# A pre-norm attention layer and a feed-forward layer on one core: work around chunk, batch and up-stage borders in another order

## The chip, the cores and the metric

The kernel runs on 1 core of one Trainium2 chip. The metric is the device time of one execution in microseconds (us), as the median of several runs. The engines are named as the profile names them: PE is TensorE (matrix products; PEld is its weight load), DVE is VectorE, ACT is ScalarE, POOL is GpSimd, and SP is SyncE, which here only issues DMAs.

## The reference

Two batches of 2048 rows of width 1024, float32 throughout. First a single-head attention layer of width 256 with a residual, then a feed-forward layer with a residual:

```python
x = x + attn(layernorm(x), Wqkv, bqkv, Wo, bo)      # qkv: 1024 -> 3*256; softmax(q k^T / 16) v; Wo: 256 -> 1024
x = x + ffn(layernorm(x), gate_w, up_w, down_w, fc1_w, fc2_w, expert_w, ln_gamma, ln_beta)
# ffn(h): relu(h @ up_w)**2 @ down_w                                   (1024 -> 2048 -> 1024)
#         + (h @ fc1_w @ expert_w * sum(top_2(h @ gate_w))) @ fc2_w    (1024 -> 512 -> 512 -> 1024)
#         then a layer norm with ln_gamma and ln_beta
```

## The kernel before, in words

Each float32 operand is split into a high half (an fp32r cast, made by ACT) and a low half (source minus high half, made by DVE or POOL, lines 1184 and 1922, called `low` on both), and PE sums three products for each operand pair (`mm3`, lines 2146 to 2148). The text calls the two halves the high half and the low half. No scheduler decides the order: the program of every engine is written out by hand, each engine takes its instructions strictly in that order, and semaphores join them (`w.wait_ge`). Every wait therefore also holds up all that stands behind it on its engine, and the same is true of SP, which issues nearly all DMAs.

**Stage 1, chunks (0 to 345 us).** The 4096 rows are taken in 8 chunks `c` of 512. For a chunk DVE computes the norm's statistics (`stats1`, `aggr1`, `diff1`, `rstd1`, with two small PE products between them, `combine1a` and `combine1b`), scales the 16 row groups (`norm1`) and transposes the chunk in eight slabs `j` (`turn1`). ACT makes the high half of a slab (`slab_hi`), DVE or POOL the low half (`slab_low`; slab 0 on DVE, slab 1 on POOL). PE multiplies the eight slabs into Q and K, then makes V in four steps `t`. Only when step 3 of V has read slab 0 may the next chunk's slab 0 be written. Next to all this run the weight sums (`prep`): 40 pieces of 512 KB are loaded, added and subtracted on DVE and POOL, and stored (`ups`, `downs`), for the fast matrix products of the feed-forward layer, which replace eight block products by seven.

**Stage 2, attention (to some 794 us).** 16 pairs `C` of 128-row tiles, `even = 2C` and `odd = 2C + 1`: scores (`s_unit`), row maxima and exponentials, a transpose on DVE (`turn_p`, `turns`), a shuffle through DMA (`shuffle`), P times V (`pv`), the output product (`wo_half`), `residual` (DVE) into the one pair of buffers `x1t`, which `store1` (SP) writes to DRAM as `x1d` and `norm2` (POOL) normalises into `x2n`, stored by `store2`. `residual` of a pair thus waits for `store1` and `norm2` of the pair before. Pairs 0 to 7 belong to one batch, 8 to 15 to the other; at C = 7 and 8 K and V of the second batch are loaded (`load_k`, `load_v`). PE's `pv(7, 0)` waits for `residual(6, 0)`, since both use PSUM bank 6.

**Stage 3, feed-forward (from 794 us).** 4 blocks `n` of 1024 rows; each has an up stage of 70 slots `s` and a down stage of 70 (60 in the last block). Each slot is twelve PE products of 512 columns, with one weight tile that goes through a ring of three: SP fetches it three slots ahead (`fetch`, into `stf`), ACT casts it, POOL makes its low half (`w_low`). In a down stage ACT and DVE (or POOL) also make the two halves of one hidden tile a slot (`hop_hi`, `hop_low`, tiles `hr`), and POOL adds hidden tiles (`h_add`, line 2006) in slots 3 to 36; in the last block DVE adds them (line 1486). The rows of the next block are loaded in two halves (`load_x2`) and transposed by DVE (`turn2`), the second half in slots 44 to 51 of the down stage. `add_beta` on POOL adds beta to the stored residual rows.

The order inside a DVE wait is what matters at most of the places; for the slab and for the PSUM bank it is:

```python
w.wait_ge(*v_turn[c, j])                 # ACT, slab_hi: the slab is transposed
if c:
    w.wait_ge(*p_v[c - 1, 3, j])         # and V, step 3, has read the slab before
...
w.wait_ge(*d_x1[i][g - 2])               # DVE, residual: the store of the pair before has landed
w.wait_ge(*g_x2[g - 2])                  # and POOL has normalised it
```

## Time and profile before

| | us |
|---|---|
| median of 3 runs (lowest, highest) | 2382.38 (2382.31, 2389.34) |
| the profiled execution's own time | 2392.45 |
| its span, first to last instruction | 2390.6 |
| PE busy, share of the span | 2319.8 (97%) |
| DVE, POOL, ACT busy | 1769.4 (74%), 1564.7 (65%), 902.2 (38%) |
| mean granted PE clock, of full speed | 0.990 |

The profile is one execution. Busy time of an engine is the time in which it has an instruction in work; an idle time in square brackets stands before an instruction and names what ended it. The granted clock of PE is given as a share of full speed: 1.0 is 2.4 GHz and 0.5 is 1.2 GHz, and a value between is a mean over a stretch. The DMA share is the mean busy share of the core's 16 DMA engines.

### The profile page before, as it was taken

Reading aid. Unit: us, or ns where it says so; the run is one execution under the profiler, and the core shown is the slowest. Engines: PE = TensorE matmul, PEld = TensorE weight load, DVE = VectorE, ACT = ScalarE, POOL = GpSimd, SP = SyncE. Lnnn points to the kernel's source line nnn. Section 1 sums busy time; section 2 is a strip of 40 time slices with the busy share of each in tenths; the row PEclk is TensorE's granted clock in tenths of the full one; section 3 lists DMA queues with packets and bytes.
Section 4 is the critical chain, followed back from the end, with each engine's and each line's share of the span. In section 5 each row is a group of like instructions: output and inputs, shape, how many; then the busy total and the mean of one; then the engine's idle time right before and its main releaser. Section 6 shows DMA issues by size and latency. Waiting matters only on the chain.

```text
span 2390.6 us, 31307 instructions
## 1 busy us (share of the span) xinstructions
PE 2319.8 (97%) x11224; PEld 1931.4 (81%) x11224; DVE 1769.4 (74%) x2952; ACT 902.2 (38%) x1698; POOL 1564.7 (65%) x1173
## 2 busy tenths in 40 slices
PE   7999999998999999999999999999999999999998
PEld 6888889987888788877887887887787778877786
DVE  5989957887887653854689875479895457989968
ACT  4222233432433353444432444442254343244352
POOL 4557525664665776598658479846649974866763
PEclk9999999999999999999999999999999999999999
DMA  9899846778767733435335343535534443544342
GB/s 244 281 308 283 255 130 194 216 216 278 220 204 215 225 115 93 124 97 146 101 117 179 106 131 92 149 95 158 149 104 117 125 115 110 181 147 131 88 139 87
DMA packets 215802, 386.48 MB, mean 162 GB/s; under 512 B 19552, under 2 KB 95456, under 8 KB 215008
## 3 DMA queue, kind: packets, MB, share of 16 engines
q1 hardware_dynamic: 214496, 382.38, 54.8%
q8 instruction: 90, 1.47, 0.3%
q10 hardware_dynamic: 1152, 2.10, 0.2%
q14 instruction: 64, 0.52, 0.1%
HBM read 260.67 MB, written 90.18 MB: 147 GB/s over the span
## 4 chain that ended last, share of the span: by engine, by line
PE 47%; DVE 24%; POOL 13%; DMA 7%; issue 6%; SPq 3%; ACT 1%; DVEq 0%; POOLq 0%; ACTq 0%
PE ps L2146 16%; PE ps L2148 15%; PE ps L2147 15%; DVE pturn L1306 5%; POOL hq L2006 4%; DMA pland<-pturn 4%; POOL wr0l L1922 2%; POOL wr2l L1922 2%; POOL wr1l L1922 2%; DVE xr L1577 2%; SPq L638 2%; DVE x L1333 1%; DVE mx L1289 1%; DVE xi L1242 1%; DVE xopAl L1184 1%
## 5 line engine op out<-in xcount | busy, mean ns | idle before, releaser
L1922 POOL TENSOR_TENSOR wr1l<-stf,wr1h 128x512 fp32r<-128x512 f32 x183 | 263.7, 1441 | 147.3 <-ACT wr1h L966 147.2
L1922 POOL TENSOR_TENSOR wr2l<-stf,wr2h 128x512 fp32r<-128x512 f32 x183 | 259.0, 1415 | 151.2 <-ACT wr2h L966 151.2
L1922 POOL TENSOR_TENSOR wr0l<-stf,wr0h 128x512 fp32r<-128x512 f32 x184 | 260.1, 1414 | 142.2 <-ACT wr0h L966 142.1
L966 ACT CAST wr1h<-stf 128x512 fp32r<-128x512 f32 x183 | 113.8, 622 | 309.3 <-PE ps L2148 242.0
L966 ACT CAST wr2h<-stf 128x512 fp32r<-128x512 f32 x183 | 113.8, 622 | 302.9 <-PE ps L2148 243.2
L966 ACT CAST wr0h<-stf 128x512 fp32r<-128x512 f32 x184 | 114.4, 622 | 296.8 <-PE ps L2148 243.9
L1922 POOL TENSOR_TENSOR pt<-pland,pt 128x512 fp32r<-128x512 f32 x120 | 152.6, 1309 | 83.8 <-ACT pt L944 83.8
L934 ACT ACTIVATE prob<-ps,nm 128x512 f32<-128x512 f32 x128 | 86.3, 687 | 253.4 <-DVE nm L1297 253.4
L1306 DVE STREAM_TRANSPOSE pturn<-prob 128x512 f32<-128x512 f32 x128 | 131.9, 1091 | 59.9 <-DMA pland<-pturn 57.4
L1184 DVE TENSOR_TENSOR hr2l<-hq,hr2h 128x512 fp32r<-128x512 f32 x78 | 97.4, 1249 | 86.3 <-ACT hr2h L985 86.3
L2146 PE MATMUL ps<-pt,vh 128*128 128x256 f32 x512 | 146.5, 286 | 10.3 <-DVE x L1333 9.0
L1184 DVE TENSOR_TENSOR hr1l<-hq,hr1h 128x512 fp32r<-128x512 f32 x78 | 92.4, 1184 | 83.1 <-ACT hr1h L985 82.9
L1184 DVE TENSOR_TENSOR hr0l<-hq,hr0h 128x512 fp32r<-128x512 f32 x78 | 94.9, 1217 | 78.5 <-ACT hr0h L985 78.4
L2147 PE MATMUL ps<-pt,vh 128*128 128x256 f32 x512 | 145.6, 284 | 0.0
L2148 PE MATMUL ps<-pt,vl 128*128 128x256 f32 x512 | 145.5, 284 | 0.0
L2006 POOL TENSOR_TENSOR hq<-hq,hq 128x512 f32<-128x512 f32 x90 | 138.9, 1544 | 0.0
L1922 POOL TENSOR_TENSOR xl<-xt,xh 128x512 fp32r<-128x512 f32 x54 | 71.3, 1330 | 69.4 <-ACT xh L924 69.4
L1968 POOL TENSOR_SCALAR x<-x,nm,rst 128x1024 f32<-128x1024 f32 x28 | 34.4, 1239 | 121.8 <-DVE rst L1198 121.8
L2146 PEld LDWEIGHTS ps<-pt,vh 128*128 128x128 f32 x512 | 98.9, 193 | 13.9 <-DVE x L1333 11.8
L2146 PE MATMUL ps<-xh,wh 128*128 128x512 f32 x256 | 102.5, 400 | 7.5 <-DVE xl L1184 7.5
L2146 PE MATMUL ps<-kh,q 128*128 128x512 f32 x256 | 101.0, 395 | 2.8 <-ACT prob L934 2.8
L2147 PE MATMUL ps<-kl,q 128*128 128x512 f32 x256 | 100.5, 393 | 0.0
(478 smaller groups left out, 7774.8 us busy)
## 6 DMA issues: line engine op xcount, KB each, us to landing
stf<-ups SPq DMA_DIRECT2D x160, 256.0 KB, 3.3
stf<-downs SPq DMA_DIRECT2D x160, 256.0 KB, 2.9
pland<-pturn SPq DMA_DIRECT2D x120, 256.0 KB, 4.7
stf<-in_upw_dram SPq DMA_DIRECT2D x120, 256.0 KB, 2.6
stf<-in_down_dram SPq DMA_DIRECT2D x88, 256.0 KB, 2.7
x<-in_x_dram SPq DMA_DIRECT2D x32, 512.0 KB, 6.5
x1d<-x SPq DMA_DIRECT2D x32, 512.0 KB, 5.6
xi<-in_x_dram SPq DMA_DIRECT2D x28, 512.0 KB, 9.9
```

The costliest lines, as they stand in the source:

```text
L638: eng.dma_start(land(g)[:, 512 * i + 32 * n * h:512 * i + 32 * n * (h + 1)], turned(g)[32 * i:32 * i + 32, :].rearrange("p (k s) -> p k s" ...
L934: eng.activation(prob[:, 512 * kb:512 * kb + 512], ps[:, kb, :], ACT.Exp, bias=nm[:, 0:1], scale=1.0 / 16, accum_out=rs[:, kb:kb + 1]).the ...
L966: eng.copy(hi, src).then_inc(*a_w.up(K))
L1184: eng.tensor_tensor(lo, src, hi.bitcast(F32), ALU.subtract).then_inc(*done)
L1306: eng.transpose(turned(g)[:, :].rearrange("p (k s b) -> p s k b", k=4, b=32)[:, 4 * kb:4 * kb + 4], prob[:, 512 * kb:512 * kb + 512].rearr ...
L1577: ins = eng.scalar_tensor_tensor(buf[:, cols], o_of(n, t, hh), rst3[:, t:t + 1], buf[:, cols], ALU.mult, ALU.add)
L1922: eng.tensor_tensor(lo, src, hi.bitcast(F32), ALU.subtract).then_inc(*done)
L1968: eng.tensor_scalar(x2n[C][i][:, :], x1t[i][:, :], nm2[:, i:i + 1], rst2[:, i:i + 1], ALU.add, ALU.mult).then_inc(*g_x2.up(g))
L2006: eng.tensor_tensor(hq[o][:, c, :], hq[a][:, c, :], hq[b][:, c, :], op).then_inc(*g_hs.up((n, name, c)))
L2146: eng.matmul(o, ah, bh, start=first, stop=False)
L2147: eng.matmul(o, ah, bl, start=False, stop=False)
L2148: return eng.matmul(o, al, bh, start=False, stop=last)
```

## The change

It moves work and changes no arithmetic. The parts, named as the prediction names them:

- **(a)** Of chunk 1's norm, ACT scales row groups 0 to 7 (`norm_rows`), DVE the other eight; DVE makes the bias for it (`nbias1`).
- **(b)** In each chunk DVE takes the low half of the next chunk's slab 0 after the transposes of V step 1, ahead of the weight sums (`prep`) and of two V low halves.
- **(c)** At C = 7 SP stores `x1d` ahead of the last four K loads, POOL does `norm2` ahead of the bias add (`xadd`), DVE takes the last moments and the first `at_low` ahead of the transposes; at C = 8 DVE takes `residual(6, 0)` first.
- **(d)** At C = 9 DVE does the first two residuals ahead of the transposes of tile 18.
- **(e)** Entry of the up stage: POOL takes `w_low(3)` and `w_low(4)` ahead of `norm2(14, 0)`, and `w_low(5)` ahead of `norm2(14, 1)`; SP fetches three weight tiles in a row and stores pair 14 in slots 1 and 2; the row loads begin at slot 3; `store1(15)` goes from slot 0 to slot 8.
- **(f)** In the down stages of blocks 0 to 2 the second half of the next block's rows is loaded in slots 20 to 23 and no longer in 39 to 42.
- **(g)** In the last block two `add_beta` go from slots 14 and 17 to 26 and 29.

Left out of the diff are the longer lists of semaphore keys, the waits on `a_norm` that go with (a), and at C = 15 two unchanged neighbours.

```diff
--- before.py
+++ after.py
...
@@ -772,9 +772,10 @@
                 if C == 7:
                     xload(C - 1)
                     shuffle(odd)
+                    store1(C - 2)
                     for kb in (2, 3):
                         load_k(kb)
-                if C >= 2:
+                if C >= 2 and C != 7:
                     store1(C - 2)
                 if C != 7:
                     xload(C - 1)
@@ -792,13 +793,11 @@
                     for k in range(3):
                         fetch(k)
                 if C == 16:
-                    fetch(3)
-                if C >= 2:
+                    for k in range(3, 6):
+                        fetch(k)
+                if 2 <= C < 16:
                     for i in range(2):
                         store2(C - 2, i)
-                if C == 16:
-                    fetch(4)
-                    fetch(5)
 
 
             def load_x1(n, t, buf):
@@ -818,16 +817,18 @@
                 for s in range(70):
                     turnover(PER * n + s)
                     if n == 0:
-                        if s in (0, 2, 4, 6):
+                        if s in (1, 2):
+                            store2(14, s - 1)
+                        if s in (3, 4, 5, 6):
                             for u in range(4):
                                 w.wait_ge(*v_stt[15, u])
                             w.wait_ge(*pt_lo(31, 2))
                             w.wait_ge(*pt_lo(31, 3))
-                            load_x2(0, 1, s // 2)
-                        if s == 0:
+                            load_x2(0, 1, s - 3)
+                        if s in (4, 5):
+                            store2(15, s - 4)
+                        if s == 8:
                             store1(15)
-                        if s in (3, 4):
-                            store2(15, s - 3)
                         if s == 12:
                             w.wait_ge(*v_tp[31, 3])
                             eng.dma_start(gam[:, :], gamma.partition_broadcast(128)).then_inc(*d_gb.up(0))
@@ -855,9 +856,9 @@
                         if s < 4:
                             w.wait_ge(*p_up[n, 69])
                             load_x2(n + 1, 0, s)
-                        if 39 <= s < 43:
+                        if 20 <= s < 24:
                             w.wait_ge(*v_t2[n + 1, 0, 7])
-                            load_x2(n + 1, 1, s - 39)
+                            load_x2(n + 1, 1, s - 20)
                         if s in (40, 45):
                             t = (s - 40) // 5
                             if n:
@@ -1007,15 +1008,17 @@
                 w.wait_ge(*a_relu.now())
                 eng.activation(h, h, ACT.Square).then_inc(*a_act.up((n, q, c)))
 
+            def norm_rows(c, gs):
+                w.wait_ge(*v_nb[c])
+                for g in gs:
+                    xg = XI[c][:, g, :]
+                    ins = eng.activation(xg, xg, ACT.Identity, bias=nb1[:, g:g + 1], scale=rst1[:, g:g + 1])
+                ins.then_inc(*a_norm.up(c))
+
 
             for k in STG[:12]:
                 stage_hi(k)
-            w.wait_ge(*v_nb[0])
-            for g in range(16):
-                if g not in NORM_DVE:
-                    xg = XI[0][:, g, :]
-                    ins = eng.activation(xg, xg, ACT.Identity, bias=nb1[:, g:g + 1], scale=rst1[:, g:g + 1])
-            ins.then_inc(*a_norm.up(0))
+            norm_rows(0, [g for g in range(16) if g not in NORM_DVE])
             stage_hi(STG[12])
             slab_hi(0, 0)
             e2_evac(0)
@@ -1039,6 +1042,8 @@
                             e2_store(lt)
                     if c == 0 and j in (3, 4):
                         stage_hi(("w", 0, j - 3))
+                if c == 0:
+                    norm_rows(1, range(8))
                 for ct in (2, 3, 0, 1):
                     hi, _, src = qk_parts(c, ct)
                     if ct >= 2 and c >= 4:
...
@@ -1234,6 +1239,10 @@
                 last = v_var[c]
                 for step in range(11):
                     last = rsqrt(step, var1[:, :], rst1[:, :], tmp1[:, :], last, v_rst.up(c) if step == 10 else None)
+
+            def nbias1(c):
+                w.wait_ge(*v_rst[c])
+                eng.tensor_tensor(nb1[:, :], nmean1[:, :], rst1[:, :], ALU.mult).then_inc(*v_nb.up(c))
 
             def norm1(c, gs):
                 w.wait_ge(*v_rst[c])
...
@@ -1635,8 +1643,9 @@
                             diff1(1)
                         if j == 6:
                             rstd1(1)
+                            nbias1(1)
                         if j == 7:
-                            norm1(1, range(16))
+                            norm1(1, range(8, 16))
                     elif c < 7:
                         if j == 0:
                             stats1(c + 1, 5, 10)
@@ -1666,12 +1675,12 @@
                     eng.scalar_tensor_tensor(lo, src, bias[:, ct:ct + 1], hi.bitcast(F32), ALU.add, ALU.subtract
                                              ).then_inc(*v_qk.up((c, ct)))
                 for t in range(4):
-                    if c < 7 and t == 3:
-                        slab_low(c + 1, 0)
                     low(v_parts(c, t), a_v[c, t], v_v.up((c, t)))
                     if c < 7 and t < 2:
                         turn1(c + 1, 2 * t)
                         turn1(c + 1, 2 * t + 1)
+                    if c < 7 and t == 1:
+                        slab_low(c + 1, 0)
                     if c < 6 and t == 3:
                         stats1(c + 2, 0, 5)
                     prep(c, 8 + t)
@@ -1717,10 +1726,18 @@
             for C in range(2, 16):
                 even, odd = 2 * C, 2 * C + 1
                 if C == 8:
+                    residual(C - 2, 0)
                     pt_low(15, 0)
                     pt_low(15, 2)
-                    residuals(C - 2)
+                    moments(C - 2, 0)
+                    for u in (1, 2, 3):
+                        residual(C - 2, u)
+                        moments(C - 2, u)
                 maxima(even)
+                if C == 9:
+                    for u in (0, 1):
+                        residual(C - 2, u)
+                        moments(C - 2, u)
                 turns(even)
                 if C == 8:
                     at_low(C - 1, 0)
@@ -1736,10 +1753,9 @@
                         moments(C - 2, u)
                     for u in (2, 3):
                         residual(C - 2, u)
+                        moments(C - 2, u)
+                    at_low(C - 1, 0)
                     turns(odd)
-                    at_low(C - 1, 0)
-                    for u in (2, 3):
-                        moments(C - 2, u)
                     at_low(C - 1, 1)
                     ln2(C - 2, *range(15))
                 elif C == 15:
...
@@ -2055,11 +2073,11 @@
                     norm2(C - 2, 0)
                     norm2(C - 2, 1)
                 pt_low(even, *range(4))
-                if C < 15 and C != 8:
-                    xadd(C - 1)
                 if C == 7:
                     norm2(C - 2, 0)
                     norm2(C - 2, 1)
+                if C < 15 and C != 8:
+                    xadd(C - 1)
             pt_low(31, 1, 3)
             norm2(13, 0)
             norm2(13, 1)
@@ -2069,8 +2087,6 @@
             for k in range(3):
                 w_low(k)
             xadd(15)
-            norm2(14, 0)
-            norm2(14, 1)
 
 
             for n in range(NBK):
@@ -2078,6 +2094,8 @@
                 for s in range(70):
                     turnover(PER * n + s)
                     if n == 0:
+                        if s in (1, 2):
+                            norm2(14, s - 1)
                         if 5 <= s < 9:
                             x_low(0, 2, s - 5)
                         if s in (3, 4):
@@ -2119,8 +2137,8 @@
                     else:
                         if s in (2, 5, 8, 11):
                             add_beta(n, 4 + s // 3, xrl[4 + s // 3])
-                        if s in (14, 17):
-                            add_beta(n, s // 3 - 2, xrl[s // 3 - 2])
+                        if s in (26, 29):
+                            add_beta(n, s // 3 - 6, xrl[s // 3 - 6])
                         if s == 59:
                             w.wait_ge(*v_fin[n, 1])
                             for t in (2, 3):
```

DVE at the end of chunk 5, before (`vl` is a low half of V, `xt` a transposed slab, `pb` a weight sum, `xl` the low half of slab 0):

```order
L1254 STREAM_TRANSPOSE xt_101<-xi_96 128x512
L1273 TENSOR_TENSOR pb_114<-pb_114 128x256
L1275 TENSOR_TENSOR pb_114<-pb_114 128x256
L1184 TENSOR_TENSOR vl<-ps,vh 128x2x128
L1278 TENSOR_TENSOR pb_114<-pb_114 128x256
L1282 TENSOR_TENSOR pb_114<-pb_114 128x256
L1184 TENSOR_TENSOR xl<-xt_98,xh 128x512
L1184 TENSOR_TENSOR vl<-ps,vh 128x2x128
```

and now:

```order
L1263 STREAM_TRANSPOSE xt_101<-xi_96 128x512
L1189 TENSOR_TENSOR xl<-xt_98,xh 128x512
L1282 TENSOR_TENSOR pb_114<-pb_114 128x256
L1284 TENSOR_TENSOR pb_114<-pb_114 128x256
L1189 TENSOR_TENSOR vl<-ps,vh 128x2x128
L1287 TENSOR_TENSOR pb_114<-pb_114 128x256
```

The low half of slab 0 has passed four weight sums and one V low half.

SP at C = 7, now (before, the two `x1d` stores stood behind the four K loads):

```order
L638 DMA pland_133<-pturn 128x1x512 x4
L657 DMA x1d<-x_128 128x1024
L657 DMA x1d<-x_129 128x1024
L667 DMA kh<-kd 128x1024
L667 DMA kl<-kd 128x1024
L667 DMA kh<-kd 128x1024
L667 DMA kl<-kd 128x1024
L622 DMA q_121<-qd 128x1024
```

The stores now come right behind the shuffle of tile 15.

POOL at the entry of the up stage, before (`x_126`, `x_127` get the bias, `x2e` is `norm2` of pair 14, `wr0l` to `wr2l` are weight low halves):

```order
L1977 TENSOR_TENSOR x_127<-x_127,bob 128x512 x2
L1968 TENSOR_SCALAR x2e_137<-x_128,nm_70,rst_68 128x1024
L1968 TENSOR_SCALAR x2e_138<-x_129,nm_70,rst_68 128x1024
L1922 TENSOR_TENSOR wr0l<-stf_217,wr0h 128x512
L1922 TENSOR_TENSOR wr1l<-stf_218,wr1h 128x512
L1922 TENSOR_TENSOR wr2l<-stf_219,wr2h 128x512
```

and now:

```order
L1995 TENSOR_TENSOR x_127<-x_127,bob 128x512 x2
L1940 TENSOR_TENSOR wr0l<-stf_217,wr0h 128x512
L1940 TENSOR_TENSOR wr1l<-stf_218,wr1h 128x512
L1986 TENSOR_SCALAR x2e_137<-x_128,nm_70,rst_68 128x1024
L1940 TENSOR_TENSOR wr2l<-stf_219,wr2h 128x512
L1986 TENSOR_SCALAR x2e_138<-x_129,nm_70,rst_68 128x1024
```

The first weight low half has passed both halves of `norm2`, the next two have passed one of them or both.

## Rows read from the trace of the kernel before

**Rows 1.** Who waited for whom, PE, whole span: idle us, times, longest.
```profile
PE ps L2146 <- DVE x L1333: 9.0, 2, 7.4
PE ps L2146 <- DVE xl L1184: 7.5, 5, 3.0
...
PE ps L2146 <- POOL wr0l L1922: 5.6, 5, 3.6
...
PE ps L2146 <- DVE vl L1184: 2.5, 1, 2.5
```

**Rows 2.** Windows: length, busy (count) of PE, PEld, DVE, ACT, POOL; clock, DMA share, GB/s.
```profile
1200.00:1250.00 50.00, 50.00 (x222) 41.42 (x221) 41.34 (x58) 18.02 (x32) 27.59 (x20) 1.00 0.35 110
```

**Rows 3.** Windows, PE alone: length, busy (count), granted clock, DMA share, GB/s.
```profile
70.00:80.00 10.00, 7.55 (x44) 0.83 0.69 256
290.00:300.00 10.00, 9.81 (x36) 0.83 0.68 217
805.00:815.00 10.00, 8.67 (x25) 0.66 0.96 313
1920.00:1925.00 5.00, 3.77 (x10) 0.67 0.68 212
```

**Rows 4.** Timeline of DVE: start us, us, line, operation, out<-in, count [idle before].
```profile
62.63 8.08 DVE L1242 TENSOR_SCALAR xi<-xi,nmean,rst 128x256 f32<-128x256 f32 x16
```

**Rows 5.** ACT's row groups of chunk 0 (line 1017): ns min/median/max.
```profile
L1017 ACT ACTIVATE xi<-xi,nb,rst x11: 583/586/600, 28.7 to 33.7; 128x256 f32<-128x256 f32 x11
```

**Rows 6.** Timelines of DVE and ACT in stage 1.
```profile
193.50 0.17 DVE L1224 TENSOR_SCALAR nmean<-ps 128x16 f32<-128x16 f32 x1 [0.65 <-PE ps L2163]
...
284.81 1.14 ACT L924 CAST xh<-xt 128x512 fp32r<-128x512 f32 x2
...
288.39 1.75 DVE L1184 TENSOR_TENSOR xl<-xt,xh 128x512 fp32r<-128x512 f32 x1
```

**Rows 7.** DMA queues, 100 to 300 us: packets, MB, share of 16 engines.
```profile
q1 hardware_dynamic: 50253, 57.97, 95.2%
```

**Rows 8.** Timelines of SP, DVE and POOL around C = 7 and 8.
```profile
537.01 0.59 SPq L667 DMA_DIRECT2D kh<-kd  x1
...
540.14 1.14 SPq L657 DMA_DIRECT2D x1d<-x  x2
...
548.47 0.75 DVE L1333 SCALAR_TENSOR_TENSOR x<-ps,rinv,x 128x512 f32<-128x512 f32 x1 [4.70 <-DMA x1d<-x]
```

**Rows 9.** Tile x1d, 530 to 556 us.
```profile
DMA to landing us min/median/max: 3.0/6.0/8.7
```

**Rows 10.** Timelines of DVE and POOL at the entry of the up stage.
```profile
790.33 10.00 DVE L1355 TENSOR_SCALAR nm<-mv 128x2 f32<-128x2 f32 x1
...
802.67 2.37 POOL L1968 TENSOR_SCALAR x2e<-x,nm,rst 128x1024 f32<-128x1024 f32 x2 [2.37 <-DVE rst L1198]
805.00 1.27 POOL L1922 TENSOR_TENSOR wr0l<-stf,wr0h 128x512 fp32r<-128x512 f32 x1
```

**Rows 11.** Who waited for whom, PE, 1500 to 1535 and 1900 to 1930 us.
```profile
PE ps L2146 <- DVE hr1l L1184: 1.4, 1, 1.4
...
PE ps L2146 <- DVE hr2l L1184: 2.0, 1, 2.0
```

**Rows 12.** Timeline of DVE, third down stage.
```profile
1919.79 0.71 DVE L1365 STREAM_TRANSPOSE xq<-xia 128x512 f32<-128x512 f32 x1 [9.44 <-DMA xia<-x2d]
```

**Rows 13.** Tile stf, 1105 to 1135 us (row loads beside it), then 1045 to 1075 us.
```profile
DMA to landing us min/median/max: 2.9/3.7/8.5
...
DMA to landing us min/median/max: 2.7/2.9/3.8
```

**Rows 14.** Who waited for whom, PE, 2215 to 2250 us.
```profile
PE ps L2146 <- DVE hr1l L1184: 2.0, 2, 1.6
PE ps L2146 <- DVE hr0l L1184: 0.8, 2, 0.4
```

**Rows 15.** Timeline of POOL, last down stage.
```profile
2226.31 3.43 POOL L2013 TENSOR_TENSOR xrz<-xrz,bet 128x512 f32<-128x512 f32 x2
```

19 lines of the change are left out of this document (10 added, 9 removed).

## The prediction

> **What bounds the kernel now.** I began with the shares of busy time: PE has an instruction in work for 97% of the span, and the change leaves PE's own program as it is, product for product. In the undisturbed middle it starts 222 products in 50 us [rows 2], 0.225 us each, so a slot of twelve is 2.7 us. What can be won is therefore only PE's idle time and its time at a low clock. Second came the list of what PE waited for, over the whole span and then stage by stage [rows 1, 11, 14]: many short waits, each for one named tile. Third came windows of PE's granted clock [rows 3], since a stall costs more than its idle time where the clock falls behind it. Fourth came the timelines of the engine named in each wait, to see what stood ahead of the late instruction in its queue [rows 4 to 6, 8, 10, 12, 15]. The reader should see seven places, each with a late tile, and ask of each what is late next.
>
> **(a) Chunk 1's norm.** DVE scales 16 row groups in 8.08 us [rows 4], 0.505 each; then come the low halves of Q, K and V step 0, and PE waited 2.5 for the last of these [rows 1]. Eight groups leave: 4.0 us sooner. ACT takes 8 x 0.586 = 4.7 us for them [rows 5], at the same time, and it was idle there; its casts of Q and K start up to 4.7 later than now, but DVE, which needs them, was 8 us away and is 4 away now. So DVE follows ACT closely and V step 0 is ready about 3 us sooner than now, which covers the 2.5. The clock over 70 to 80 us was 0.83 [rows 3], 1.7 us lost over 10 us; that goes too. Against it, the low half of slab 0 of chunk 1 now waits for ACT's casts: I charge 0.5. **3.7.**
>
> **(b) The chunk borders.** PE waited five times for `xl`, 7.5 us in all, 3.0 the longest [rows 1]. At the longest one ACT had the first high half after half of 1.14 us, at 285.4, and DVE did the low half from 288.39 to 290.14 [rows 6]. Set right behind the transposes it starts at 285.4 and, at the same 1.75, ends 3.0 us sooner: the whole wait. At the others less was missing and the same order holds, so all 7.5 go, and with them the clock loss of 290 to 300 us, 0.83, 1.7 us. What is late next: DVE's work is the same but PE comes sooner, 1.5 us a border. DVE had slack where it waits for PE's statistics product, at the least 0.65 us, in chunk 4 [rows 6]; there PE now waits for DVE, 1.5 - 0.65 = 0.8. **9.2 - 0.8 = 8.4.** The head of DVE's queue may now wait for ACT's cast with weight sums behind it; they are not due within the chunk, and in chunk 7 DVE is idle for long, so this costs nothing. Its cover is that idle time; without it, it would be up to 2 us a chunk.
>
> **(c) C = 7 and 8.** PE waited 7.4 for `residual(6, 0)` (the longest for `x` in [rows 1]). DVE itself had waited 4.70 for the store of `x1t`, issued at 540.14, behind four K loads that began at 537.01; it landed at 548.4, 8.3 after its issue [rows 8]. Issued in the loads' place, some 0.6 later than 537.0 since two moments now stand ahead of the transposes, it lands 3.0 to 8.7 us later [rows 9]; I take the middle value, 6.0, since only the shuffle is ahead of it: 543.6. `residual` (0.75) and one low half of P (about as long) follow, which was made before the wait until now: PE goes on at 545.1, not 549.2. **4.1**, with 1.4 for a landing of 8.7 and 5.5 as the other end, where POOL's `norm2` and bias add, which both must be done, decide. The clock loss stays.
>
> **(d) C = 9.** The shorter of the two waits for `x`, 9.0 - 7.4 = 1.6 [rows 1]. DVE stands idle for the shuffle just then, and the two residuals now fill that idle time. **1.6.**
>
> **(e) Entry of the up stage.** PE waited 3.6 for `w_low(3)`, of the 5.6 of that row [rows 1], and the clock was 0.66 over the next 10 us [rows 3], 3.4 lost: 7.0 in all. `w_low(3)` stood behind `norm2(14)`, 802.67 to 805.0, which waited 2.37 for DVE; and DVE's tiny instruction before it took 10.00 us, to 800.3 [rows 10], just as long as POOL worked without a pause. Now `w_low(3)` runs at 800.3 to 801.6, in time for slot 3 at 802.7. `w_low(4)` follows to 802.9, and if DVE stays locked out until then, its root ends 2.4 later (800.3 to 802.67), at 805.3, `norm2(14, 0)` at 806.5, and `residual(15, 0)`, which frees slot 4's bank, at 807.3. Slot 4 is due at 805.4: 1.9 us of new stall. Behind it `norm2(15)` now stands ahead of `w_low(7)` with DVE just done, so about the same lateness shows once more or is hidden by the lower clock. I leave half of the 7.0, and take the other 3.5 less 0.5. **3.0**, between 1 and 7.
>
> The Trainium skill (SBUF — State Buffer, "Who interferes with whom") says that DVE and GpSimd share a port pair by an exclusive lock held for one instruction, the loser blocked until it ends. By that, DVE would wait one POOL instruction (1.3 us) and not 10.00; the row shows a wait through several in a row, so the row decides. By the page the new stall would not be there and the sum would be 4 us larger; this is the second rival.
>
> **(f) Rows 19 slots sooner.** DVE waited 9.44 for the rows [rows 12], with low halves of hidden tiles behind it; PE waited 1.4 in block 1 and 2.0 in block 2 [rows 11], and in block 2 the clock was 0.67 over 5 us, 1.7 lost. Loaded 21 slots ahead of use they are there: 5.1. What the loads meet now: slots 20 to 26, where POOL adds hidden tiles without a pause. Beside row loads a weight tile landed after 3.7 us (8.5 at most), without them after 2.9 [rows 13]. The ring gives three slots, 8.1 us, for landing, cast (0.57 [rows 6]) and low half (1.27 [rows 10]), so up to 6.3 us costs nothing. Some will exceed it: I charge 0.3 a block, 1.0. **4.1**, between 0 and 5.1.
>
> **(g) The last block.** DVE's low halves were late by 2.0 + 0.8 us [rows 14]. An `add_beta` on POOL takes 3.43 us there [rows 15], two instructions, and each delays one of DVE's by the 1.0 us between 1.75 [rows 6], a low half beside POOL, and 0.75, an operation of that size alone [rows 8]. Two `add_beta` gone are 4 x 1.0 = 4.0 us for DVE, more than it was late. The first of the waits, 0.4, is before them. **2.4**, and at slots 26 and 29 DVE has one hidden sum fewer a slot and can bear them; nothing on SP, ACT or PE's path hangs on these `add_beta` before the end.
>
> **Sum.** 3.7 + 8.4 + 4.1 + 1.6 + 3.0 + 4.1 + 2.4 = 27.3 us. The profiled execution took 2392.45, 10 above the median of the runs; nearly all of what is counted is waits of a fixed order, so I take the same 27 off the median: 2382.4 - 27 = **2355**. From no change a measurement of this kernel can tell about 0.3%, 7 us.
>
> **Rivals.**
> 1. *The stalls only move.* Behind each late tile stands another one: in (b) the statistics, in (c) the low half of P, in (e) the root. For it: DVE is busy for nearly all of stage 1. Against it: the waits after the late tile are short everywhere. Half of the sum goes: 14 less, 2368.
> 2. *The lock is held for one instruction only*, DVE gets through between two of POOL's: (e) gives 7.0, the sum is 31, 2351. Against it stands the 10.00 us row.
> 3. *The DMA queues bind stage 1.* They are 95.2% busy from 100 to 300 us [rows 7], so of 200 us 9.6 are spare and (b) asks for 8.4 of them. If POOL's weight sums come late for it, its low halves do too, and two thirds of (b) come back: 21.5, 2361.
> 4. *Slower: the weight ring starves in (f).* If in each of three blocks three tiles land at the 8.5 us of [rows 13], 2.2 beyond the 6.3 that are free, PE waits 2.2 and, at stalls of that size, loses 1.7 by the clock: 9 x 3.9 = 35 us. Without (f) the sum is 23, so 12 slower: 2394. It decides from a landing of 6.3 us on. Against it: only the tiles issued among the last row loads landed so late, with two loads of `xr` beside them, which are elsewhere now.
> 5. *A part does nothing:* if the store in (c) lands as late as before, 4 are missing. That lies within the range.
>
> **Chances.** Forecast 0.58 (own range 2350 to 2361), rival 1 0.14, rival 2 0.09, rival 3 0.14, rival 4 0.02; 0.03 stay for what I don't see, without a sign. The range takes in rivals 2 and 3 and most of 1, and the bounds of (c), (e) and (f) together (+2.7 + 3.1 + 4.1 up, -1.4 - 4.0 - 1.0 down, not all at once): 2345 to 2370. Faster by over 7 us: all but rival 4, the rest and the tail of rival 1: 0.93. Same 0.05, slower 0.02.
>
> **What would show it.** In the list of PE's waits `xl` should be under 1.5 us, `vl` and `hr1l` of block 1 and `hr2l` of block 2 gone, the longest `x` some 3.3; `wr0l` near 802 gone, with a wait for `x` of some 2 us near 805 in its place. The granted clock over 70 to 80 and 290 to 300 should be 1.0. DVE should wait for no `xia`. In slots 20 to 26 of the down stages the waits of PE for `wr` must not grow by more than 1 us in all. I am wrong if PE's waits fall and the span doesn't, if `xl` stays over 3 us, or if a wait for `wr` over 2 us appears in a down stage.

## The result and the profile after

| | before | changed |
|---|---|---|
| median of the runs of the first comparison, us | 2383.42 | 2365.05 |
| lowest, highest | 2382.31, 2389.34 | 2362.46, 2370.4 |
| the profiled execution's own time, its span | 2392.45, 2390.6 | 2362.46, 2360.7 |
| PE busy | 2319.8 | 2309.0 |

The ratio is 0.9921, with a 95% interval of 0.9897 to 0.9945; in a second comparison (below) it is 0.9933 (0.9917 to 0.995). The kernel is 16 to 18 us faster. 27 were forecast: the time lies inside the range, 10 us above the value. The two profiled executions, though, are 29.9 us of span apart, more than forecast. That is the riddle of this case: the sum was about right for the trace it was made from, and for the kernel a third of it was missing.

Who waited for whom, PE in the changed kernel, whole span (idle us, times, longest):

```profile
PE ps L2181 <- DVE mv L1218: 6.5, 3, 4.5
PE ps L2164 <- DVE pt L1189: 5.3, 2, 4.7
...
PE ps L2164 <- POOL wr1l L1940: 3.4, 3, 1.6
...
PE ps L2164 <- DVE xl L1189: 2.8, 4, 0.7
...
PE ps L2164 <- DVE x L1342: 2.2, 2, 2.0
...
PE ps L2164 <- DVE hr2l L1189: 1.1, 3, 0.5
```

Against [rows 1]: `vl` is gone, `xl` fell from 7.5 to 2.8, the longest `x` from 7.4 to 2.0; DVE's `hr` waits of [rows 11] are gone too (no `hr` wait here is over 0.61). New are `mv` within stage 1, which is the statistics of the next chunk (of its 6.5 us 4.5 are the start-up, where the kernel before waited 6.3), `pt`, at C = 7, and `wr1l` at 1.6. The clock was full in the windows that answer to the first three of [rows 3] (length, busy and count, granted clock, DMA share, GB/s):

```profile
70.00:80.00 10.00, 9.31 (x51) 1.00 1.03 365
290.00:300.00 10.00, 10.00 (x45) 1.00 0.61 209
795.00:805.00 10.00, 8.37 (x37) 1.00 0.53 147
```

The new waits, in order. In chunk 6 the statistics of chunk 7, on DVE and PE:

```profile
256.62 1.17 DVE L1218 BATCH_NORM_AGGREGATE mv<-st 128x2 f32<-128x6 f32 x16
...
257.84 0.41 PE L2181 MATMUL ps<-mv,quad 128*128 128x32 f32 x2 [1.40 <-DVE mv L1218]
```

At C = 7 (DVE, POOL, PE):

```profile
532.43 0.75 DVE L1342 SCALAR_TENSOR_TENSOR x<-ps,rinv,x 128x512 f32<-128x512 f32 x1 [6.80 <-DMA x1d<-x]
533.10 3.43 DVE L1189 TENSOR_TENSOR pt<-pland,pt 128x512 fp32r<-128x512 f32 x2
...
533.03 2.95 POOL L1940 TENSOR_TENSOR pt<-pland,pt 128x512 fp32r<-128x512 f32 x2
...
535.00 0.55 PE L2164 MATMUL ps<-pt,vh 128*128 128x256 f32 x1 [4.68 <-DVE pt L1189]
```

The store had landed after 6.0 us (issued at 526.23), but the low half of P behind `residual(6, 0)` ran beside POOL's own low halves of P and took 1.75, not 0.75 (the line shows two of them, 3.43 together). At the entry of the up stage (DVE, POOL, PE):

```profile
774.23 12.51 DVE L1364 TENSOR_SCALAR nm<-mv 128x2 f32<-128x2 f32 x1
...
785.43 1.28 POOL L1940 TENSOR_TENSOR wr1l<-stf,wr1h 128x512 fp32r<-128x512 f32 x1
789.08 1.20 POOL L1986 TENSOR_SCALAR x2e<-x,nm,rst 128x1024 f32<-128x1024 f32 x1 [2.37 <-DVE rst L1203]
...
790.42 0.75 DVE L1342 SCALAR_TENSOR_TENSOR x<-ps,rinv,x 128x512 f32<-128x512 f32 x1 [1.45 <-POOL x2e L1986]
...
791.32 0.47 PE L2164 MATMUL ps<-xop01h,wr1h 128*128 128x512 f32 x1 [1.96 <-DVE x L1342]
...
798.90 1.20 POOL L1986 TENSOR_SCALAR x<-x,nm,rst 128x1024 f32<-128x1024 f32 x1 [4.94 <-DVE rst L1203]
...
801.39 0.50 PE L2164 MATMUL ps<-xop01h,wr1h 128*128 128x512 f32 x1 [1.63 <-POOL wr1l L1940]
```

Here all came as worked out: DVE's tiny instruction stands from 774.23 until POOL's first pause at 786.7, the root ends 2.4 later, `norm2(14, 0)` and `residual(15, 0)` follow, and PE waits 1.96 for it at slot 4 (1.9 forecast) and 1.63 at slot 7.

**Stretch by stretch.** PE's program is the same in all these kernels, so the start of one and the same product can be compared between traces. The table gives by how much each stretch is shorter than in the first trace of the kernel before, in us, worked out from the starts of PE's products; its borders are times of that first trace. All but its first column belong to the experiments below.

| stretch (part) | changed | before, again | changed, again | (a,c,e,g) alone | (b,d,f) alone |
|---|---|---|---|---|---|
| 0 to 27 | 1.6 | -0.5 | 0.5 | 0.3 | 1.2 |
| 27 to 78 (a) | 3.7 | 0.4 | 4.5 | 3.4 | 0.4 |
| 78 to 328 (b) | 4.6 | 2.6 | 4.4 | 3.7 | 5.8 |
| 328 to 520 | 1.3 | 0.5 | 1.3 | -0.1 | 0.2 |
| 520 to 575 (c) | 2.5 | -1.0 | 4.1 | 3.4 | -0.9 |
| 575 to 620 (d) | 1.5 | 0.0 | 1.2 | -1.8 | 2.0 |
| 620 to 760 | 0.4 | 0.2 | 0.5 | 0.7 | 0.1 |
| 760 to 856 (e) | 2.4 | -0.8 | 1.8 | 3.1 | 0.9 |
| 856 to 1928 (f) | 8.8 | 3.5 | 6.3 | 6.1 | 6.4 |
| 1928 to 2215 | 1.4 | -1.6 | 0.8 | 0.9 | -0.9 |
| 2215 to 2290 (g) | 1.6 | 0.0 | 1.6 | 1.6 | 0.0 |
| rest | 0.4 | 0.2 | 0.0 | 0.1 | 0.2 |
| sum | 30.0 | 3.5 | 26.9 | 21.4 | 15.5 |

### The profile page after: what moved, and what is told of

Its sections match the earlier page's. It is cut to its first block, busy times and chain, and to the rows that moved or that the text cites. A ratio compares the mean times of both kernels' runs of the same rounds, so it can differ in the third digit from the quotient of the medians.

```text
span 2360.7 us, 31308 instructions
## 1 busy us (share of the span) xinstructions
PE 2309.0 (98%) x11224; PEld 1926.0 (82%) x11224; DVE 1773.2 (75%) x2945; ACT 906.2 (38%) x1706; POOL 1571.0 (67%) x1173
## 4 chain that ended last, share of the span: by engine, by line
PE 50%; DVE 21%; POOL 15%; DMA 6%; issue 5%; SPq 2%; ACT 1%; DVEq 0%; POOLq 0%; ACTq 0%
PE ps L2164 17%; PE ps L2166 16%; PE ps L2165 16%; POOL hq L2024 5%; DVE pturn L1315 5%; DMA pland<-pturn 4%; POOL wr1l L1940 2%; POOL wr2l L1940 2%; POOL wr0l L1940 2%; SPq L638 2%; DVE mx L1298 1%; DVE x L1342 1%; DVE hq L1495 1%; DMA stf<-ups 1%; DVE xi L1251 1%
## 5 line engine op out<-in xcount | busy, mean ns | idle before, releaser
L1189 DVE TENSOR_TENSOR hr1l<-hq,hr1h 128x512 fp32r<-128x512 f32 x78 | 98.0, 1257 | 85.6 <-ACT hr1h L986 85.5
L2165 PE MATMUL ps<-xl,wh 128*128 128x512 f32 x256 | 99.8, 390 | 0.0
```

Of the source, the lines that this page charges most:

```text
L1189: eng.tensor_tensor(lo, src, hi.bitcast(F32), ALU.subtract).then_inc(*done)
L2165: eng.matmul(o, ah, bl, start=False, stop=False)
```

## The experiments

Twelve runs were made, in four groups, two of them of the unchanged kernels; each was timed in five rounds against the kernel before on the same chip.

### Both kernels again

No edit.

> The kernel before, unchanged, traced a second time. The two traces shown so far differ by 29.9 us of span, the medians only by 18.4, and the first trace of the kernel before lay 9 us above its median. Theory A (a few waits differ from execution to execution): this trace is some 8 us shorter than the first one and the shortness sits in places that the change does not touch (the start, the clock behind the wait near 345 us, single waits of 0.4 to 1.2 us in the up stages), while the seven waits that the change is aimed at are there again with nearly the same lengths (vl 2.5, xl 7.5 in five, x 7.4 and 1.6, wr0l 3.6, hr1l and hr2l in blocks 1 and 2 1.4 and 2.0). Theory B (the waits aimed at are themselves a matter of chance): at least two of them are missing or under half their length here.

> The changed kernel, unchanged, traced a second time. Against the kernel before in the same rounds: 18 to 20 us faster. Theory A: its waits at the places of the change come out again (xl four times 0.69, mv 0.67 and 1.40 in stage 1, pt 4.7 near 530, x 1.96 and wr1l 1.63 at the entry of the up stage). Theory B: they come out elsewhere.

Measured: the kernel before 0.9999 (0.9987 to 1.0011) against itself, 2382.26 and 2382.89 us, its 34 runs in this group between 2378.36 and 2391.38; the changed kernel 2366.47, ratio 0.9933 (0.9917 to 0.995). PE's waits in the second trace of the kernel before:

```profile
PE ps L2146 <- DVE x L1333: 9.9, 2, 8.2
PE ps L2146 <- DVE xl L1184: 5.2, 4, 2.4
```

The trace is 3.5 us shorter than the first, not 8. Theory A holds for most waits and B for three: the `xl` wait at chunk 7's border, the longest of [rows 1] with 2.96, is absent (four are left, 5.2 in all), and so is the 2.0 us for `hr2l` in block 2 [rows 11]; the 1.44 of block 1 is 0.51. The two that are absent had a low clock behind them, 1.7 us each. But the second trace has low clocks of its own. One stands behind the `xl` wait near 254 us, which is 2.42 long here and was 1.82 in the first trace, with the clock at 1.00 behind it (PE, second trace):

```profile
250.00:260.00 10.00, 7.58 (x31) 0.83 0.97 316
```

So the 2.6 us of the table's third column are mostly 3.0 + 1.7 less 0.6 and 1.7, and no edit made them. The two other traces with the old order of (b), `r3_aceg` and `s4_no_b` below, show the same four waits, 5.2 in all, with the same 0.83 behind the one of 2.42: the wait at 290 us stands in one trace of four, a clock loss of 1.7 behind the longest `xl` wait in all four. The 3.5 us of the feed-forward stretch are such a balance too: against the missing waits, one for `hr0l` at 1022.6 is 2.28 for 1.05, with a low clock behind it. In the changed kernel the waits of stage 1 and of the entry came out again within 0.1, but for one `xl` that was missing; `pt` at C = 7 was 3.46 for 4.68, with DVE's first low half of P at 0.82 for 1.75, and `pt` near 760 us was 2.20 for 0.65.

Why the wait at 290 was there in one trace only is to be read on DVE. First trace, DVE and POOL:

```profile
286.14 1.46 DVE L1278 TENSOR_TENSOR pb<-pb 128x256 f32<-128x256 f32 x1
287.86 0.61 DVE L1282 TENSOR_TENSOR pb<-pb 128x256 f32<-128x256 f32 x1
...
286.03 1.29 POOL L1922 TENSOR_TENSOR xl<-xt,xh 128x512 fp32r<-128x512 f32 x1 [9.12 <-ACT xh L924]
287.28 0.91 POOL L1948 TENSOR_TENSOR pb<-pb 128x256 f32<-128x256 f32 x1
```

Second trace, DVE and POOL:

```profile
286.94 0.42 DVE L1278 TENSOR_TENSOR pb<-pb 128x256 f32<-128x256 f32 x1
287.94 0.68 DVE L1184 TENSOR_TENSOR xl<-xt,xh 128x512 fp32r<-128x512 f32 x1
...
288.24 1.54 POOL L1922 TENSOR_TENSOR xl<-xt,xh 128x512 fp32r<-128x512 f32 x1 [9.89 <-ACT xh L924]
```

The same instructions, the same order. In the first trace POOL began its low half 2.2 us sooner and then worked beside DVE: a weight sum took 1.46 for 0.42, `xl` 1.75 [rows 6] for 0.68. POOL had waited for ACT's high half in both; what made that early in the one trace and late in the other I have not followed.

### The change in two halves

`r3_aceg` is the kernel before with the hunks (a), (c), (e) and (g) of the change's diff, `r4_bdf` with (b), (d) and (f); of the hunk at C = 8 and 9 each has its own half:

```diff
 r4_bdf, on the kernel before
+                if C == 9:
+                    for u in (0, 1):
+                        residual(C - 2, u)
+                        moments(C - 2, u)
                 turns(even)
```

> The changed kernel with parts (b), (d) and (f) undone. If each wait is local, the parts add up: by the first two traces (a) gives 4.1, (c) 3.1, (e) 1.9 and (g) 2.1 us, together 11, so this kernel is some 11 us faster than the kernel before and some 8 slower than the changed one; the xl waits of the chunk borders are back at some 7 us. Rival (stalls only move): what one part wins is lost at the next one, and this kernel stands within 4 us of the changed one or of the kernel before.

> The kernel before with parts (b), (d) and (f) alone. If each wait is local: (b) 3.9, (d) 1.6, (f) 3 to 5, together 9 to 10 us faster than the kernel before, and its gain and that of the kernel with (a), (c), (e) and (g) make up the gain of the whole change within 3 us. Rival (stalls only move): the two gains do not add up. Weight ring (rival 4 of the prediction): waits for wr of more than 2 us in slots 20 to 26 of the down stages.

Measured: 2368.58 us, ratio 0.9942 (0.9929 to 0.9955), 14 faster; and 2378.97, ratio 0.9974 (0.9963 to 0.9986), 4 to 6 faster. The gains make 18 by the medians and 20 by the ratios, against 16 for the whole in this group: they add up within 2 to 4, so stalls do not just move from part to part. But the halves are not the sizes expected: the first gave 14 for 11, the second 4 to 6 for 9 to 10. No wait for `wr` over 0.5 us appeared in a down stage of blocks 0 to 2, in any kernel here or below: the weight ring (rival 4) never starved.

### One part undone: (b), (f)

```diff
 s4_no_b, on the changed kernel
+                    if c < 7 and t == 3:
+                        slab_low(c + 1, 0)
                     low(v_parts(c, t), a_v[c, t], v_v.up((c, t)))
...
-                    if c < 7 and t == 1:
-                        slab_low(c + 1, 0)
 t3_no_f, on the changed kernel
-                        if 20 <= s < 24:
+                        if 39 <= s < 43:
```

> The changed kernel with (b) alone undone. By the prediction (b) is worth 8.4 us. By the four traces of the kernel before and of the two halves of the change it is worth about 3: the longest xl wait, 2.96 with 1.7 of lost clock behind it, was there in one trace of the kernel before and in no other kernel with the old order, and 2.07 of new mv waits come with (b). So: 1 to 4 us slower than the changed kernel; xl waits of 0.69 to 2.4 in four places, none at chunk 7's border, no mv wait.

> The changed kernel with (f) alone undone: rows loaded in slots 39 to 42 again. By the prediction 4.1 us slower. The waits on which that rested, 1.44 in block 1 and 1.97 with 1.7 us of clock in block 2, were 0.51 and absent in the second trace of the kernel before, so I expect 1 to 3 us: waits for hr or for DVE of 0.5 to 1.5 us near slots 44 to 51 in one or two of the three blocks, and DVE waits of 4 to 9 us for xia in all three.

Measured: without (b) 2368.59, ratio 0.9947 (0.9928 to 0.9965), by the medians 2 to 4 us behind the changed kernel, though the intervals overlap; without (f) 2365.54, ratio 0.9928 (0.9913 to 0.9943), no difference. PE's waits between 60 and 320 us without (b), then in the second trace of the changed kernel (its first trace has four `xl` waits there, 2.8 in all):

```profile
PE ps L2164 <- DVE xl L1189: 5.2, 4, 2.4
```
```profile
PE ps L2164 <- DVE xl L1189: 2.1, 3, 0.7
PE ps L2181 <- DVE mv L1218: 2.1, 2, 1.4
```

(b) trades 5.2 us of `xl`, and the 1.7 us of low clock behind the longest of them, for 2.1 to 2.8 of `xl` and 2.1 of `mv`, with no low clock: 2.0 to 2.7 us. Without (f) DVE waited for the rows as before, and PE hardly felt it:

```profile
1893.19 0.71 DVE L1374 STREAM_TRANSPOSE xq<-xia 128x512 f32<-128x512 f32 x1 [7.62 <-DMA xia<-x2d]
...
1894.62 0.47 PE L2164 MATMUL ps<-wr2h,hr2h 128*128 128x512 f32 x1 [0.80 <-DVE hr2l L1189]
```

In blocks 0 and 1 DVE waited 6.42 and 6.86. Only the third wait reached PE, with 0.80. Over the four traces without (f) PE loses nothing where DVE waits up to 6.9 us, up to 0.8 at 7.5 to 8.1, and 1.3 to 2.0 at 8.3 to 9.5 [rows 12]; with the one low clock behind such a wait that is 5.1 us in the first trace and 0.5, 1.9 and 0.8 in `r1`, `r3` and `t3`. (f) is worth what the landing of the rows happens to be.

### What ate the gain of (b)

```diff
 s3_lean, on the changed kernel, in DVE's prep
-                    a = [pb[i % 5][:, x, :] for x in range(4)]
+                    a = [pb[i % 5][:, x, 0:16] for x in range(4)]
```

> The changed kernel with DVE's weight sums on 16 of 256 columns, so that part of the weight sums is left out and DVE has some 30 to 40 us less to do over stage 1; DMAs and POOL's share stay. What ate the gain of (b) is either DVE's own load behind the border or the DMA queues. DVE theory: the mv waits of 0.67 and 1.40 in chunks 2 and 5 go, while the xl waits of 0.69 stay, since only transposes stand ahead of them; the kernel is 2 to 3 us faster than the changed one. DMA theory (rival 3 of the prediction): DMA share over 100 to 300 us is as high as before and the mv waits stay; time as the changed kernel.

This kernel leaves out 15 of 16 columns of DVE's sums. Measured: 2358.65, ratio 0.99 (0.9884 to 0.9915), 6 to 8 us under the changed kernel; from 78 to 328 us 10.0 shorter than the first trace of before, where the changed kernel is 4.6. PE's only wait in stage 1 behind the start, the DMA queues from 100 to 300 us (packets, MB, share), and DVE's weight sums from 80 to 300 (count, busy us, mean ns), there and in the changed kernel:

```profile
PE ps L2164 <- DVE xl L1189: 0.7, 1, 0.7
...
q1 hardware_dynamic: 49551, 57.82, 94.1%
...
L1291 DVE TENSOR_TENSOR pb<-pb 128x16 f32<-128x16 f32 x13 | 9.3, 719 | 0.2
L1287 DVE TENSOR_TENSOR pb<-pb 128x16 f32<-128x16 f32 x13 | 8.1, 620 | 0.2
```
```profile
q1 hardware_dynamic: 48813, 56.55, 92.9%
...
L1291 DVE TENSOR_TENSOR pb<-pb 128x256 f32<-128x256 f32 x13 | 11.8, 909 | 0.2
L1287 DVE TENSOR_TENSOR pb<-pb 128x256 f32<-128x256 f32 x13 | 10.2, 781 | 0.2
```

The `mv` waits (they stood in chunks 3 and 6) are gone with the DMA share at 94.1%, no lower than the 92.9% of the changed kernel: DVE's own load binds, not the DMA queues, and rival 3 falls. Three of the four `xl` waits went as well, against the expectation, so they were more than the order of the transposes. And a sixteenth of the columns takes still nearly four fifths of the time of these two lines, 620 and 719 ns for 781 and 909. Over all 52 sums of stage 1 DVE saved 10.6 us, not 30 to 40. In the changed kernel 42 of the 52 have a POOL instruction beside them and take 0.90 us in the mean, the ten others 0.41; in the lean kernel it is 0.74 and 0.17. About half of what the sums cost DVE is thus not the sum but the wait beside POOL. POOL gained as well, 4 us on its own sums, so the relief was not DVE's alone; the kernels below that move sums from DVE to POOL are the test of that.

What the order of (b) costs can be read from the same sums. DVE's busy time with them from 80 to 345 us (count; clock, DMA share, GB/s), without (b) and in the changed kernel:

```profile
80.00:345.00 265.00, 35.29 (x52) 0.99 0.87 260
```
```profile
80.00:345.00 265.00, 42.00 (x52) 1.00 0.86 258
```

The first number behind the window's length is the busy time. It is 35.2 to 35.7 in the four traces with the old order and 40.9 to 42.7 in the five with the order of (b) and full sums: behind the border more of them stand beside POOL (29 of 52 without (b), 42 with it). Moving `xl` forward so made DVE's work some 6 us longer, which no count of slack had in it.

### Three orders altered, and the entry alone

```diff
 s1_all, on the changed kernel
+                    if c < 7 and t == 1:
+                        slab_low(c + 1, 0)
                     if c < 7 and t < 2:
                         turn1(c + 1, 2 * t)
                         turn1(c + 1, 2 * t + 1)
-                    if c < 7 and t == 1:
-                        slab_low(c + 1, 0)
...
+                    store1(C - 2)
                     shuffle(odd)
-                    store1(C - 2)
...
+            x_low(0, 1, 0)
+            x_low(0, 1, 1)
             at_low(15, 0)
...
             for k in range(3):
                 w_low(k)
-            xadd(15)
+            norm2(14, 0)
+            norm2(14, 1)
+            xadd(15, 0)
 s2_lock, on the changed kernel
-            for k in range(3):
-                w_low(k)
+            w_low(0)
+            norm2(14, 0)
+            w_low(1)
+            norm2(14, 1)
+            w_low(2)
             xadd(15)
```

In `s1_all` the two `x_low` are DVE's, POOL keeps j = 2 and 3; `xadd(15, 1)`, the bias add of tile 31, comes in slot 1. In both, `norm2(14)` no longer stands in slots 1 and 2.

> The changed kernel with three orders altered. Borders: the low half of slab 0 goes ahead of the second pair of transposes, not behind it. PE waited 0.69 us for it up to four times although ACT had the high half some 1.2 us before DVE began. Theory: all four xl waits go (2.8 us). Rival (stalls only move): the transposes are late in their place and PE waits about as long for a later slab. C = 7: SP issues the x1d stores ahead of the shuffle, so residual(6, 0) waits for POOL's bias add alone; the wait for pt near 535, 4.68 and 3.46 us in two traces, falls to 1.5 to 2.5. Entry of the up stage: DVE makes two of the four low halves of xop01, POOL then does both norm2 of pair 14 ahead of the bias add. Theory (DVE is locked out as long as POOL works without a pause): DVE's tiny instruction, 12.5 us long in three traces of the changed order, now ends at POOL's first pause, after at most 4 us, and the waits x 1.96 and wr1l 1.63 go. Rival (the tiny instruction waits for something else at the entry): it still ends some 12 us after its start and these waits stay. Together 5 to 8 us faster than the changed kernel, 21 to 25 faster than the kernel before; by the rivals 2 or less.

> The changed kernel with POOL made to pause at the entry of the up stage: norm2(14, 0), which waits for DVE, stands between the first and the second weight low half, norm2(14, 1) behind the second. Lock theory: DVE's tiny instruction, 12.5 us long and ended by POOL's first pause in three traces, is now 2 to 3 us long, since POOL stops after one weight low half; POOL waits some 2.4 us for the rest of the root, so PE waits up to 2 us at slot 1, and the waits x 1.96 and wr1l 1.63 go. Rival (a lock held for one instruction only, and something else ends the tiny instruction 12.5 us later): it stays that long, and POOL and then PE stand still for about 10 us more than now. By the lock theory the time is within 2 us of the changed kernel, by the rival some 10 slower.

Measured: 2357.36, ratio 0.9895 (0.9878 to 0.9912), 8 to 9 us under the changed kernel, the fastest of all; and 2365.28, ratio 0.9934 (0.9919 to 0.9949), as the changed kernel.

In `s1_all` all `xl` waits went, and `mv` waits of 0.74, 2.60 and 0.75 came, with a low clock behind the 2.60: the stretch is 4.0 us shorter than in the first trace, where the changed kernel has 4.4 to 4.6. At the borders, then, the rival was right, stalls only moved. At C = 7 `residual(6, 0)` no longer waited for its store, but `pt` was 3.44, as in the second trace of the changed kernel: the shuffle, issued until 528.1, landed at 533.6, and that is the next bound there. What the trace shows of the gain is at the entry, where both waits went (760 to 856 us: 5.6 shorter, 2.4 and 1.8 in the changed kernel). That is 3 to 4 of the 8 to 9 us; the rest has no place that I can name, since the traced execution, 2360.99, was the slowest of its five.

In `s2_lock` the tiny instruction took 2.50 us and ended with POOL's pause, to the tenth (DVE, then POOL):

```profile
778.64 2.50 DVE L1364 TENSOR_SCALAR nm<-mv 128x2 f32<-128x2 f32 x1
...
779.82 1.29 POOL L1940 TENSOR_TENSOR wr0l<-stf,wr0h 128x512 fp32r<-128x512 f32 x1
783.48 1.20 POOL L1986 TENSOR_SCALAR x2e<-x,nm,rst 128x1024 f32<-128x1024 f32 x1 [2.38 <-DVE rst L1203]
```

It also had its cost: `w_low(3)` came behind the bias add and PE waited 2.9 for it. The rival, that something else at the entry held the instruction, falls.

### Best parts together

```diff
 t1_mix, on the changed kernel
-                    if i % 3 != 2:
+                    if i % 4 != 3:
                         continue
...
+            at_low(15, 0)
             x_low(0, 1, 0)
             x_low(0, 1, 1)
-            at_low(15, 0)
...
-                        if s in (26, 29):
+                        if s in (40, 43):
```

The first edit gives DVE its pieces of the weight sums, the second is against the entry of `s1_all`, which is otherwise kept, the third moves the two `add_beta`. `t2_mix_border` is `t1_mix` with `slab_low` ahead of the second pair of transposes. `u1_best` is `s1_all` without its edit of `store1`, with the first edit of `t1_mix`.

> The changed kernel with three edits. DVE takes every fourth piece of the weight sums, not every third (10 of 40, 13 until now), POOL the rest; at the entry of the up stage DVE makes two of the four low halves of xop01 (behind the last but one low half of the attention output, so that this is not 1.6 us late again) and POOL does norm2 of pair 14 ahead of the bias add; the two add_beta go from slots 26 and 29 to 40 and 43, where DVE adds no hidden tiles. If DVE's load in stage 1 is what ate the gain of (b): with about a quarter of the relief of the kernel with lean weight sums (which won 4.5 us over stage 1 and lost both mv waits) the mv wait of 1.40 falls and stage 1 is 1 to 3 us shorter. Entry: 3 us as in the kernel with all three orders, and 1 more without the late atl. add_beta: the slots of 2.9 us from 2245 on go, 1.0 to 1.6 us. Together 5 to 8 us faster than the changed kernel: 22 to 26 faster than the kernel before. Rival (stalls only move): POOL now is late with its low halves of slabs, and stage 1 is no shorter.

> The kernel of t1 with the low half of slab 0 ahead of the second pair of transposes. In the kernel with DVE's full load this took away four xl waits of 0.69 and brought mv waits of 0.74, 2.60 and 0.75, for nothing in all. If DVE's load is what brings the mv waits, then with less load some of the 2.8 us stays: 1 to 2 us faster than t1. If the order alone brings them, it is as t1.

> The changed kernel with the edits that won in their own stretch: DVE with every fourth piece of the weight sums, the low half of slab 0 ahead of the second pair of transposes (stage 1 was 3.4 us shorter with these two than in the second trace of the changed kernel), and the entry of the up stage as in the kernel with all three orders, DVE's two low halves of xop01 ahead of at_low, norm2 of pair 14 ahead of the bias add (2 us net there); add_beta and C = 7 as in the change. If the stretches add up: 5 us under the changed kernel and about 3 under the kernel with all three orders, 27 to 29 faster than the kernel before. If a DVE instruction is held back through a run of POOL instructions at the entry, as the low halves of xop01 were for 10.6 us in t2, up to 8 of it go again.

Measured: 2365.63, ratio 0.9929 (0.9912 to 0.9946); 2363.38, ratio 0.9924 (0.9908 to 0.9941); 2360.51, ratio 0.9905 (0.9888 to 0.9921). `t1` is a miss. `t2` is 2 us under it, as expected if DVE's load counts, but the intervals overlap, and `u1` is the 5 us under the changed kernel but 3 above `s1_all`, not under it. Stage 1 was a gain in `t1` and `t2` (78 to 328 us: 6.9 and 7.7 shorter than in the first trace, for 4.4 to 4.6), with POOL busier by some 8 us, which speaks for DVE's load. But it was none in `u1` (4.8), with the same order and the same split as `t2`: an `mv` wait of 2.68, with a low clock behind it, came in chunk 5. What differs between these two executions I don't know. The two `add_beta` in slots 40 and 43 saved 1.8 us at 2250 and then cost 3.6 near 2307. And in `t2` DVE needed 10.61 us at the entry for two low halves of 128x512, 10.00 of them for the first, which ended when POOL had paused (DVE, POOL, PE):

```profile
761.85 10.61 DVE L1189 TENSOR_TENSOR xop01l<-xq,xop01h 128x512 fp32r<-128x512 f32 x2
...
760.11 5.05 POOL L1997 TENSOR_TENSOR x<-x,bob 128x512 f32<-128x512 f32 x4
770.04 1.26 POOL L1942 TENSOR_TENSOR wr2l<-stf,wr2h 128x512 fp32r<-128x512 f32 x1
...
774.60 0.76 PE L2168 MATMUL ps<-woh,ath 128*128 128x512 f32 x1 [7.78 <-DVE x L1342]
```

In `t1`, with the same order, the same two took 3.07. `s1_all` stays the best version, some 25 us under the kernel before; its interval overlaps that of `u1`.

## Why the prediction was right, and where it was wrong

The places and the mechanisms were right, and the direction; a third of the sum was missing in the kernel. For each part the stretches of the table can be compared with the part in (changed, changed again, its own half) and without it (before, before again, the other half), three traces each:

| part | forecast | mean with less mean without | seen |
|---|---|---|---|
| (a) | 3.7 | 3.9 - 0.3 = 3.6 | `vl` gone, clock 1.00 |
| (b) | 8.4 | 4.9 - 2.1 = 2.8 | `xl` 2.1 and `mv` 2.1 left |
| (c) | 4.1 | 3.3 + 0.6 = 4.0 | `pt` in place of `x` |
| (d) | 1.6 | 1.6 + 0.6 = 2.2 | wait gone |
| (e) | 3.0 | 2.4 - 0.0 = 2.4 | waits of 1.96 and 1.63 |
| (f) | 4.1 | 7.2 - 3.2 = 4.0; by t3 nothing | DVE's wait gone, PE's was chance |
| (g) | 2.4 | 1.6 - 0.0 = 1.6 | 3.4 won, 1.8 given back |

(a), (c) and (d) hold. In (c) the landing of 6.0 was right, the low half more than twice as long as put (1.75), and the wait for the store had been longer in the other traces (8.20 for 7.43). (e) held to the tenth at slot 4, and "about the same lateness shows once more", which I left open, is the 1.63 at slot 7; in `r3_aceg` and `s3_lean` a low clock came behind slot 4 instead and that wait is absent, the other half of the same sentence. The row of (f) is mostly scatter: its stretch is 1072 us long, and without (f) it is 9.4 us shorter in `t3` and 6.1 in `r3`, with it 5.4 to 9.4. In (g) "one hidden sum fewer a slot and can bear them" was the wrong half-sentence: at slot 26 DVE has one hidden sum, as at slot 14; between 2230.6 and 2239.2 us of the changed kernel three low halves and two hidden sums take 1.74 to 1.78 us each beside POOL, for 0.68 alone, and the change gives back 1.8 of its 3.4 us there.

**The step that failed first is the size of (b)**, 8.4 forecast and 2.8 seen, in two pieces. "All 7.5 go, and with them the clock loss" was priced from one execution: its wait of 3.0 at 290 us is in none of the three other traces with the old order, which have 5.2 us of `xl` and 1.7 of low clock. That takes 2.3 off. And "DVE had slack where it waits for PE's statistics product, at the least 0.65": what is left is `xl` 2.1 for nothing forecast and `mv` 2.1 for 0.8, another 3.4. The slack was counted, but not that the four weight sums and the low half of V which `xl` overtakes are now done behind it, while PE already runs, and that the sums become longer there (42.0 us for 35.3). In chunk 6 DVE stood idle for 2.26 us before PE's statistics in the first trace, and PE waited 1.40 all the same. DVE is busy for 192 to 201 of the 220 us from 80 to 300 in the four traces with the old order and for 204 to 208 in the five with (b). The lean kernel, with 10.0 us won in the stretch for 4.6, shows the missing part to be real and mostly DVE's.

**The second is the sentence "nearly all of what is counted is waits of a fixed order, so I take the same 27 off the median".** The profiled execution lay 10 us above its median, and that excess sat partly in the waits that I counted. Priced from the second trace by the same steps, (b) is 5.2 + 1.7 - 0.8 = 6.1, and (f) is the 0.5 that is left for `hr1l` less the charge of 1.0, nothing: 27.3 would have been 21, and 18.4 and 16.4 were measured. What of the rest of the excess is in a typical execution isn't shown: both traced executions of the kernel before (2392.45 and 2388.94) were slower than their medians.

Of the signs, `xl` fell to 2.8, not under 1.5, and DVE still waits 1.6 to 2.5 us three times for `xia`, the first half of the rows, which costs PE nothing, and the wait left at C = 7 stands on `pt` with 4.7, not on `x` with 3.3; the others came. Two sums of the prediction don't come out, without weight for it: two thirds of (b) off leave 21.7, not 21.5, and from 3.0 down to 1 is 2.0 for (e), not 3.1.

Of the rivals, the first, stalls only move, is true of the borders alone and in its number (2368) near the result by way of them. The second and the Trainium skill's rule are weighed below. The third falls with the lean kernel, the fourth with the weight ring's waits.

## What to carry to other kernels

Before a gain is summed from waits, trace the same kernel a second time: waits that come out again to the tenth (here `vl`, the shorter `xl`, `wr0l`) are the order's, and those that don't are chance, with the clock loss behind them; a profile that lies above its median is likely to hold some. Ask of an instruction that is moved forward what it overtakes, and when that is due: on an engine at 92% the overtaken work is the next stall. And where two engines slow each other, count instructions and not only their size: a sixteenth of the columns still took 31.4 of 42.0 us here, and the same sums took 35 or 42 us depending on what stood beside them.
